# A graph update with its two scratch arrays laid side by side: one load per group instead of two, eight load slots, u in its own buffer of four, distances in place

## The reference, cut to what matters

```python
h = max(layernorm(x), 0)                            # (50000, 128)
m = relu(concat(h[src], h[dst], edge_attr) @ Wm1 + bm1)
messages = relu(m @ Wm2 + bm2)                      # (25000, 128)
agg = segment_sum(messages, dst, 50000)
u = relu(concat(h, agg) @ Wu1 + bu1)
out = x + h + (u @ Wu2 + bu2)
```

## Time and profile before

| | us |
|---|---|
| median of 3 runs | 803.32 |
| the runs | 797.92, 803.32, 805.46 |
| the profiled execution, its own time | 801.2 |
| its span, first to last instruction | 799.4 |
| mean granted TensorE clock | 0.994 of full speed |
| VectorE busy | 676.6 (85%) |
| TensorE busy | 696.8 (87%) |
| ScalarE busy | 630.2 (79%) |
| GpSimd busy | 560.2 (70%) |
| HBM read, written | 107.25 MB, 76.98 MB |

### The profile page before, as it was taken

How to read it: one execution, slowest core, us unless ns; L and a number is a source line. 1 busy time by engine, 2 the same in 40 slices (tenths; PEclk the granted TensorE clock), 3 DMA queues, 4 the chain that set the end, 5 groups by cost and what they waited for, 6 DMA issues and landing times.

```text
span 799.4 us, 18691 instructions
## 1 busy us (share of the span) xinstructions
PE 696.8 (87%) x3158; PEld 416.1 (52%) x3159; DVE 676.6 (85%) x2269; ACT 630.2 (79%) x1434; POOL 560.2 (70%) x784
## 2 busy tenths in 40 slices
PE   0499999998898888888888888879999999999997
PEld 0244444444444444434444444445777787776775
DVE  3698898988898888888888888749999999989886
ACT  0588888888788888888778888846787888888886
POOL 7777777777777777777777777429887666555553
PEclk9999999999999999999999999999999999999999
DMA  6466666666666656666556665540578999999998
GB/s 153 119 212 218 221 229 218 218 214 215 211 221 214 202 197 214 214 211 208 194 196 207 217 217 187 192 161 14 161 228 266 329 349 348 354 346 352 359 351 297
DMA packets 99728, 184.57 MB, mean 231 GB/s; under 512 B 15101, under 2 KB 16512, under 8 KB 99700
## 3 DMA queue, kind: packets, MB, share of 16 engines
q1 hardware_dynamic: 46628, 81.69, 30.5%
q10 hardware_dynamic: 40528, 76.89, 27.0%
q0 software_dynamic: 12544, 25.72, 12.1%
HBM read 107.25 MB, written 76.98 MB: 230 GB/s over the span
## 4 chain that ended last, share of the span: by engine, by line
DMA 41%; issue 20%; PE 16%; POOL 6%; DVE 5%; ACT 5%; DVEq 2%; ACTq 1%; POOLq 1%; SPq 1%
DMA xg<-x_in,ends_all 38%; POOL xg L267 5%; PE bank L834 5%; PE bank L868 4%; PE bank L835 4%; DVE hot L724 2%; ACT high L780 2%; ACT dist L789 1%; POOL low L692 1%; ACT zn L452 1%; DVE hu_i L747 1%; DMA b_out<-bu_in 1%; DVE xh_o L758 1%; DMA extremes_scratch<-ext 1%; DVEq L668 1%
## 5 line engine op out<-in xcount | busy, mean ns | idle before, releaser
L267 POOL DMA_INDIRECT xg<-x_in,ends_all x392 | 388.7, 991 | 119.9 <-DMA xg<-x_in,ends_all 104.5
L692 POOL TENSOR_TENSOR low<-msgs,high 128x128 fp32r<-128x128 f32 x303 | 153.6, 522 | 93.7 <-ACT high L780 90.3
L452 ACT ACTIVATE zn<-xn,shift,rstd 128x128 f32<-128x128 f32 x392 | 160.5, 483 | 2.0 <-DVE shift L372 1.8
L724 DVE TENSOR_SCALAR hot<-node,dst_f,minus_base 128x512 fp32r<-128x512 f32 x229 | 131.1, 616 | 18.6 <-PE bank L835 8.9
L834 PE MATMUL bank<-hot,low 128*128 128x512 f32 x303 | 137.6, 454 | 9.2 <-POOL low L692 3.7
L330 DVE BATCH_NORM_STATS2 bn<-xg 128x6 f32<-128x128 f32 x392 | 80.5, 277 | 52.2 <-DMA xg<-x_in,ends_all 52.1
L835 PE MATMUL bank<-hot,high 128*128 128x512 f32 x303 | 120.4, 397 | 0.0
L540 PE MATMUL bank<-ident,xg 128*128 128x128 f32 x392 | 64.8, 289 | 55.4 <-DVE xg L395 55.4
L556 PE MATMUL bank<-ht,w_uh 128*128 128x512 f32 x196 | 106.1, 623 | 2.2 <-ACT ht L469 1.6
L395 DVE TENSOR_SCALAR xg<-xg,rstd,shift 128x128 f32<-128x128 f32 x392 | 107.1, 353 | 0.0
L868 PEld LDWEIGHTS bank<-w_out,u_t 128*128 128x128 f32 x784 | 99.2, 191 | 14.3 <-issue 6.8
(11 more groups left out here) (74 smaller groups left out, 1002.5 us busy)
## 6 DMA issues: line engine op xcount, KB each, us to landing
hu_i<-hu_scratch SPq DMA_DIRECT2D x98, 256.0 KB, 4.3
xh_i<-xh_scratch SPq DMA_DIRECT2D x98, 256.0 KB, 4.4
out<-xh_o SPq DMA_DIRECT2D x97, 256.0 KB, 4.3
hu_scratch<-ht ACTq DMA_DIRECT2D x48, 512.0 KB
xh_scratch<-xh_o ACTq DMA_DIRECT2D x48, 512.0 KB
xn<-x_in ACTq DMA_DIRECT2D x44, 512.0 KB, 3.7
xg<-x_in,ends_all POOLq DMA_INDIRECT x392, 2.7
edge<-edge_t_in ACTq DMA_DIRECT2D x45, 64.0 KB, 3.5
```

Of the source, the lines that this page charges most:

```text
L267: pool.indirect_dma_start(xg[:, slot, t, :], None, x, bass.IndirectOffsetOnAxis(ap=ends_all[:, s, t:t + 1], axis=0), engine_sem=s_made).th ...
L452: ins = act.activation(zn[:, slot % 2, t - 8, :], xn[:, slot, t - 8, :], ACT.Relu, bias=shift[:, slot % 2, t:t + 1], scale=rstd[:, slot % ...
L692: return pool.tensor_tensor(low[:, at, :], msgs[:, k, :], high[:, at, :].bitcast(F32), ALU.subtract)
L724: return dve.tensor_scalar(hot[:, at, :], node[:], dst_f[:, bass.ds(k, 1)], minus_base[:, bass.ds(g, 1)], ALU.subtract, ALU.is_equal)
```

## The change

One scratch `hx_scratch` of (98, 128, 2, 512) takes the place of the two; hu and xh of a group lie side by side, 4 KB per partition. The first phase stores to it in runs of 2 KB as before, at a pitch of 4 KB. One transfer of 512 KB in runs of 4 KB loads both. There are eight slots: four in `hx_i`, four in `ht`, which is free once the last first-layer message sums are done. SyncE loads groups 0 to 3 where it did, groups 4 to 7 right after the last stores and sums of the first phase, and group g+4 when group g-4 is finished. VectorE writes hu + sum into `u_t` (now four deep) and waits for the output sums of group g-4 before; ScalarE's relu works in place there and waits for VectorE alone. ScalarE's distance goes straight into `hot` and its wait on the previous one-hot is gone. VectorE's and SyncE's loops are unrolled eight times.

```diff
-        hu_d = nc.dram_tensor("hu_scratch", (GROUPS, P, W), F32).ap()
-        xh_d = nc.dram_tensor("xh_scratch", (GROUPS, P, W), F32).ap()
+        hx_d = nc.dram_tensor("hx_scratch", (GROUPS, P, 2, W), F32).ap()
...
-        hu_i, xh_i = sb("hu_i", [P, 4, W]), sb("xh_i", [P, 4, W])
+        hx_i = sb("hx_i", [P, 4, 2, W])
...
+        def hx(slot, k):
+            at = hx_i if slot < 4 else ht.rearrange("p a (s k) w -> p (a s) k w", k=2)
+            return at[:, slot % 4, k, :]
+
+        def load(sp, g, slot):
+            at = hx_i if slot < 4 else ht.rearrange("p a (s k) w -> p (a s) k w", k=2)
+            sp.dma_start(at[:, slot % 4], hx_d[g]).then_inc(s_ld[slot], 16)
...
-                eng.dma_start(hu_d[bass.ds(2 * s, 2)].rearrange("g p f -> p g f"), ht[:, half, 2:4]
+                eng.dma_start(hx_d[bass.ds(2 * s, 2), :, 0, :].rearrange("g p f -> p g f"), ht[:, half, 2:4]
...
-                eng.dma_start(xh_d[bass.ds(2 * s, 2)].rearrange("g p f -> p g f"), xh_o[:, half]
+                eng.dma_start(hx_d[bass.ds(2 * s, 2), :, 1, :].rearrange("g p f -> p g f"), xh_o[:, half]
...
-            u_t = sb("u_t", [P, 2, W], on=two)
-            dist = sb("dist", [P, W], on=two)
+            u_t = sb("u_t", [P, 4, W], on=two)
...
+                sp.wait_ge(s_m1, STEPS)
+                for g in range(4, 8):
+                    load(sp, g, g)
+
                 def body(g, slot, use):
-                    if at_least(g, 3) and below(g, GROUPS - 1):
-                        sp.wait_ge(s_ut, g - 2)
-                        load_hu(sp, g + 1, (slot + 1) % 4)
-                    if below(g, GROUPS) and at_least(g, 4):
+                    if at_least(g, 4) and below(g, GROUPS - 4):
                         sp.wait_ge(s_fin, g - 3)
-                        load_xh(sp, g, slot)
+                        load(sp, g + 4, (slot + 4) % 8)
                     if at_least(g, 4):
-                        store(g - 4, slot)
+                        store(g - 4, slot % 4)
-
-                run_steps(sp, GROUPS + 4, 4, GROUPS, 4, body)
+                run_steps(sp, GROUPS + 4, 8, GROUPS - 8, 8, body)
...
                     dve.wait_ge(s_agg, g + 1)
-                    dve.wait_ge(s_ldh[slot], 16 * use + 16)
-                    dve.tensor_tensor(hu_i[:, slot, :], p_agg[slot][:], hu_i[:, slot, :], ALU.add).then_inc(s_pre_u, 1)
+                    dve.wait_ge(s_ld[slot], 16 * use + 16)
+                    if at_least(g, 4):
+                        dve.wait_ge(s_o, g - 3)
+                    dve.tensor_tensor(u_t[:, slot % 4, :], p_agg[slot % 4][:], hx(slot, 0), ALU.add).then_inc(s_pre_u, 1)
...
                     dve.wait_ge(s_o, g + 1)
-                    dve.wait_ge(s_ldx[slot], 16 * use + 16)
...
-                run_steps(dve, GROUPS + 4, 8, GROUPS, 4, body)
+                run_steps(dve, GROUPS + 4, 8, GROUPS, 8, body)
...
                             act.wait_ge(s_rel, count)
-                            if at_least(g, 1):
-                                act.wait_ge(s_hot_a, count - 1)
-                            act.activation(dist[:], node[:], ACT.Abs, bias=place[:, slot:slot + 1], scale=-1.0
-                                           ).then_inc(s_dist, 1)
+                            act.activation(hot[:, at, :], node[:], ACT.Abs, bias=place[:, slot:slot + 1],
+                                           scale=-1.0).then_inc(s_dist, 1)
...
-                            act.activation(hot[:, at, :], dist[:], ACT.Relu, bias=ones[:], scale=-1.0
+                            act.activation(hot[:, at, :], hot[:, at, :].bitcast(F32), ACT.Relu, bias=ones[:], scale=-1.0
...
                     act.wait_ge(s_pre_u, g + 1)
-                    if at_least(g, 2):
-                        act.wait_ge(s_o, g - 1)
-                    act.activation(u_t[:, slot % 2, :], hu_i[:, slot, :], ACT.Relu).then_inc(s_ut, 1)
+                    act.activation(u_t[:, slot, :], u_t[:, slot, :], ACT.Relu).then_inc(s_ut, 1)
```

More of the change, by code:

```diff
@@ L110, in build @@
         s_sto = [sem(f"scratch_stored{i}") for i in range(2)]
-        s_ldh = [sem(f"hu_loaded{i}") for i in range(4)]
-        s_ldx = [sem(f"xh_loaded{i}") for i in range(4)]
+        s_ld = [sem(f"hx_loaded{i}") for i in range(8)]
         s_hot, s_hot_x = sem("first_onehots_ready"), sem("more_onehots_ready")
@@ L241, in sync_1 @@
                 for g in range(4):
-                    load_hu(sp, g, g)
-                    load_xh(sp, g, g)
+                    load(sp, g, g)
                 store_hu(sp, STEPS - 1, (STEPS - 1) % 2)
@@ L745, in add_w_h @@
                     dve.wait_ge(s_agg, g + 1)
-                    dve.wait_ge(s_ldh[slot], 16 * use + 16)
-                    dve.tensor_tensor(hu_i[:, slot, :], p_agg[slot][:], hu_i[:, slot, :], ALU.add).then_inc(s_pre_u, 1)
+                    dve.wait_ge(s_ld[slot], 16 * use + 16)
+                    if at_least(g, 4):
+                        dve.wait_ge(s_o, g - 3)
+                    dve.tensor_tensor(u_t[:, slot % 4, :], p_agg[slot % 4][:], hx(slot, 0), ALU.add).then_inc(s_pre_u, 1)
                 def finish(g, slot, use):
                     dve.wait_ge(s_o, g + 1)
-                    dve.wait_ge(s_ldx[slot], 16 * use + 16)
                     if at_least(g, 4):
-                        dve.wait_ge(s_out[slot], 16 * use)
+                        dve.wait_ge(s_out[slot % 4], 32 * use + 16 * (slot // 4))
                     elif not at_least(g, 1):
@@ L757, in finish @@
                             dve.wait_ge(s_sto[half], 32 * ((STEPS + 1 - half) // 2))
-                    dve.tensor_tensor(out_o[:, slot, :], p_out[slot][:], xh_i[:, slot, :], ALU.add).then_inc(s_fin, 1)
+                    dve.tensor_tensor(out_o[:, slot % 4, :], p_out[slot % 4][:], hx(slot, 1), ALU.add).then_inc(s_fin, 1)
                 def body(g, slot, use):
                     if below(g, GROUPS):
-                        onehots(g, slot)
+                        onehots(g, slot % 4)
                     if at_least(g, 2) and below(g, GROUPS + 2):
-                        add_w_h(g - 2, (slot - 2) % 4, use - (slot < 2))
+                        add_w_h(g - 2, (slot - 2) % 8, use - (slot < 2))
                     if at_least(g, 4):
-                        finish(g - 4, slot, use - 1)
-                run_steps(dve, GROUPS + 4, 8, GROUPS, 4, body)
+                        finish(g - 4, (slot - 4) % 8, use - (slot < 4))
+                run_steps(dve, GROUPS + 4, 8, GROUPS, 8, body)
             def scalar_2(act):
@@ L867, in outs @@
                     for j in range(4):
-                        ins = pe.matmul(to[:, j * D:(j + 1) * D], u_t[:, slot % 2, j * P:(j + 1) * P],
+                        ins = pe.matmul(to[:, j * D:(j + 1) * D], u_t[:, slot, j * P:(j + 1) * P],
                                         w_out[:], start=True, stop=True)
```

## The result

The changed kernel took 803.22 us (median of 20 runs, 799.62 to 807.58) against 801.06 us for 20 runs of the kernel before beside it: a ratio of 1.0032, 95% interval 1.0016 to 1.0047. It is slower by about 2.2 us. 2.2 us less was forecast. The profiled execution took 799.62 us (span 797.8), the shortest of its 20, so its trace shows what the change does to the work but little of where the 2 us are lost; that took the experiments.

The account below looks back on a forecast made before the run. VectorE, then a round of four engines, was taken to set the second phase's pace, with loads in time. Terms 0.5 + 0.5 + 0.8 + 0.4 = 2.2 us took the profiled 801.2 to 799.0, about 801.0 as median; range 789 to 810.

Parts of the forecast that it names:

- What bounds the kernel: Second phase: transfer engines full yet in time; VectorE sets the pace, later a round of VectorE, ScalarE, GpSimd and TensorE.
- rival A: From 640 us the transfers set the pace; 9 to 12 us less, about 792 us; chance 0.20.
- Early groups, u buffer: Groups 4 to 7 loaded in the hole before 560 us, and u four deep: 0 on the path each.
- Distances in place: ScalarE's distance passes: the new output type costs nothing; bounded at +-1.5 us over 74 passes.
- The wait near the end: VectorE's one wait for a load, 0.59 us, goes away; 0.5 us taken as gain.
- two queue items: ScalarE loses two items ahead of its register read every fourth group; at most 1.0 us, 0.5 taken.
- unrolling: VectorE's loop by eight halves its turns, seen only in waits for "issue"; at most 1.5 us, 0.8 taken.
- 4 KB runs: Loads in 4 KB packets, at 28 ns per packet, save 0.11 us DMA time per group; 0 on the path.
- C: Rival: 4 KB runs still cut into 2 KB packets; 0.4 us less gain, 801.5 us; chance 0.10.
- SyncE's order: SyncE issues two transfers a round instead of three, the store behind 512 KB instead of two 256 KB: equal.
- Register reads: ScalarE's 16 reads from 640 us shorten by 5% of 531 ns with less DMA time; 0.4 us less.
- Rival B: 512 KB transfers lengthen ScalarE's register reads beyond GpSimd's `place` cover; about 8 us more, 811 us; chance 0.12.

Follow-up runs that it names:

- e12: Kernel before with plain loads for the gathers, plus the whole change except the joint scratch, so two 256 KB loads per group; 777.47 us.
- e5: Kernel before with GpSimd's gathers replaced by plain loads of consecutive rows; 777.17 us.
- e9: Same kernel as e5 (kernel before, plain loads for the gathers), run again as a base on another chip; 776.05 us.
- e14: Changed kernel with plain loads for the gathers, each group's load split into two 256 KB transfers from the same joint scratch; 776.87 us.
- e16: Same kernel as e5 (kernel before, plain loads for the gathers), run again as a base; 777.21 us.
- e13: Same kernel as e6 (whole change, plain loads for the gathers), run again; 779.92 us.
- e6: Changed kernel with GpSimd's gathers replaced by plain loads of consecutive rows; 780.03 us.
- e15: Changed kernel with plain loads for the gathers, scratch laid out so one 512 KB transfer moves 2 KB runs; 778.51 us.
- the split: Changed kernel, gathers kept, each group loaded by two transfers in 2 KB runs from the joint scratch; 803.04 us, 0.9997 of the kernel before.
- e18: Changed kernel, gathers kept, run again beside the split; 803.70 us, 1.0017 of the kernel before.
- e1: Kernel before with only hu and xh side by side in one scratch, loads as before; 908.41 us beside 914.28, ratio 0.9924.
- e4: Whole change with the two scratch arrays of before, so two 256 KB loads per group; 915.69 us beside 914.28, ratio 0.9937.
- e2: Kernel before with only VectorE's second loop unrolled by eight; 912.59 us beside 914.28, ratio 0.995.

## Why the prediction was wrong

The range held the time (803.2 in 789 to 810) and the direction was wrong. The price of the load form was wrong with it, and that the time fell into the range is no merit of the sum: the range is 21 us wide and holds the unchanged kernel as well. Step by step:

- **What bounds the kernel: right.** The loads are not waited for although their share is 1.0, and rival A fell with it: the pace of the groups did not rise when 2.1 MB moved ahead.
- **Early groups, u buffer: right** at nothing. Their waits vanish and no time comes. Distances in place: the bound of 1.5 us can't be narrowed much; e12 has them and stands 0.3 us above e5 and 1.4 above e9.
- **The wait near the end, two queue items, unrolling: right in kind, not seen in the time.** The waits shrank as said (load 0.6 to none, VectorE's "issue" 3.0 to 1.8), which should be worth 1.8 us with my sizes. e12 and e14 have all of it, and they stand 0.7 and 0.1 us above the mean of the three bases e5, e9 and e16 (776.81). So it is worth nothing that can be measured. The step that summed them on the path is not borne out. In the changed kernel's trace the idle time removed on one engine stands as a wait for another; that it must be so in such a round is my reading, and no run tests it.
- **4 KB runs: mis-sized.** 6 ns per packet instead of 28 in the changed kernel's trace, and less than nothing in e13. From 640 to 760 us, e13 and then e14:

```profile
q1 hardware_dynamic: 14870, 40.54, 98.6%
```

```profile
q1 hardware_dynamic: 23200, 42.25, 100.0%
```

Of 1920 us these are 46.7 us per MB with 4 KB runs and 45.4 with 2 KB. The equation took its other line from the first 30 us of the kernel, where other transfers are under way; why its result is too high no run shows. It made no difference on the path, since I had taken 0 there. C is out: the packets did merge. The Trainium skill (Perfetto Trace Analysis, DMA Optimizations) says that batching small transfers, from 2 KB to 4 KB for instance, can improve throughput dramatically where a kernel with high HBM utilization is bound by DMA. No trace here shows a gain from runs of 4 KB, in a kernel that does not wait for its loads: 355 GB/s in e14 with 2 KB runs, 356 in the changed kernel with 4 KB, with shares of 1.00 and 0.99. Of the two figures of the Trainium skill (DMA: Bandwidth & Descriptors) that I cited for rival A, the stretches from 640 us on agree with the limit of about 358 GB/s (343 to 356 in the changed kernel; single slices of 20 us reach 366), without showing that it is what limits them, and no slice of 20 us comes near 408.7; no run has a load stream alone.
- **The failed step is that the form of the load was priced at nothing on the path: "Equal" in "SyncE's order", and 0.4 us less in "Register reads".** One transfer of 512 KB in place of two of 256 KB costs 3.0 us (e13 against e14, which differ in nothing else). I let the reads shorten with the DMA's busy share. The share did not fall. ScalarE's reads did shorten, from 19.5 to 24.2 us in sum to 17.4 to 19.2, several times the 0.4 us, and no time came of it: GpSimd's reads lengthened in some executions, and they stand ahead of `place` on the round. I had written that this chain covers ScalarE's read, and did not ask what covers GpSimd's. Rival B had the direction and, as the runs without gathers say, the 512 KB transfer as the cause. It had the wrong engine and size: the price is 2 to 3 us, not 8.

What is shown: the form of the load costs the time (e13 against e14, with no overlap of their six runs each; e12 beside e6 agrees, on another chip). What is seen in the traces and not tested by itself: that the longer reads of GpSimd are the way it costs. They fall into the same groups as the lost time, but no experiment moved that read alone, and a read could in part be long because the whole round had shifted against the transfers. What stays open: whether the size of the transfer or its 4 KB runs does it (e15 is between), how much of the loss is the lower clock at the start of the second phase, and why one profiled execution of the changed kernel goes through untouched, at 799.62 us, while the other three show the loss.

The version to keep is that of the kernel before or the split; neither beats the other by what can be measured (0.9997).

## What to carry to other kernels

When a transfer is not waited for, making it larger bought nothing here and cost 2 to 3 us. Look for what runs beside it, above all small reads with an uncovered latency on an engine that others wait for (the candidate here, seen and not isolated), and check each such read for its own cover, on every engine. Idle times of a few tenths of a microsecond, removed on engines that run in a round with others, should be put at zero until the last engine of the round is named. A few microseconds in 800 were told apart here with 6 runs of a kernel whose noisy part was replaced by a steady one, and hardly with 12 of the whole.

## What the runs showed of the hardware

- A register read of eight values takes GpSimd 0.57 us at the median even with the transfer engines full (e16). Among its reads 8 to 24 the longest is 1.39 us in e6, 1.37 in e13, 1.27 in e15, 1.18 in e18 and 1.06 in the changed kernel, all with loads of 512 KB, and 0.84 to 1.09 us in the thirteen traces with loads of 256 KB. Single reads early in the second phase are longer whatever the load (2.20 us in e1, 1.37 in e4).
- At a share of 0.99 to 1.01, packets of 4 KB bring no more than packets of 2 KB: 335 to 356 GB/s (e13, changed kernel) against 351 to 355 (before, e14) in the stretches shown.
- TensorE's granted clock reached 2.4 GHz for the first time between 33 and 49 us after the start, with the same instructions ahead (in e1 and e2, on the chip with the long first phase, at 55 us). At the change of phases TensorE waits 2.45 us for its first operands in all eighteen traces; in nine of them a stretch of 3.4 us at 1.2 GHz begins just there, in the others none. e9 from 508.6 to 512 us, with the clock before the DMA share (0.58 is a mean: the clock fell at 509.2 us):

```profile
508.60:512.00 3.40, 2.92 (x7) 2.38 (x8) 0.00 (x0) 1.13 (x4) 2.44 (x6) 0.58 0.00 0
```

It comes in traces of the kernel before (before, e9) and of the changed one, and where it comes the first add starts about 1 us later after ScalarE's first read (23.6 to 24.0 us in the nine, 22.6 to 22.8 in the others).
